# Last block of a four-layer kernel: routing rows loaded whole behind each tile's weights, another order of low parts at the changes of pass, a smaller first split

## The reference, cut to what matters

```
def _L1_ffn_ref(hidden_states, gate_weight, gate_up_weights, down_weights, shared_gate_up, shared_down):
    ...
    scores = jax.nn.softmax(x @ gate_weight.T, axis=-1)
    topk_weight, topk_idx = jax.lax.top_k(scores, TOP_K)
    y = jnp.zeros_like(x)
    for e in range(N_EXPERTS):
        w_e = jnp.sum(jnp.where(topk_idx == e, topk_weight, 0.0), axis=-1)
        y = y + w_e[:, None] * _glu_ffn(x, gate_up_weights[e], down_weights[e])
    y = y + _glu_ffn(x, shared_gate_up, shared_down)
```

## Time and profile before

| | |
|---|---|
| median of 3 runs | 1177.15 us (1173.48 to 1182.71) |
| the profiled execution | 1173.77 us |
| its span | 1172.0 us |
| PE busy | 1062.4 us (91%) |
| DVE, ACT, POOL busy | 782.4 (67%), 678.9 (58%), 519.9 us (44%) |
| mean granted TensorE clock | 0.966 of full speed |

### The profile page before, as it was taken

How to read it: one execution, slowest core, us unless ns; L and a number is a source line. 1 busy time by engine, 2 the same in 40 slices (tenths; PEclk the granted TensorE clock), 3 DMA queues, 4 the chain that set the end, 5 groups by cost and what they waited for, 6 DMA issues and landing times. The chain is left out here.

```text
span 1172.0 us, 18701 instructions
## 1 busy us (share of the span) xinstructions
PE 1062.4 (91%) x6437; PEld 816.3 (70%) x6437; DVE 782.4 (67%) x1801; ACT 678.9 (58%) x1240; POOL 519.9 (44%) x491
## 2 busy tenths in 40 slices
PE   7999999979998958499899999999789999878997
PEld 5422323246877957498799899889689787666997
DVE  6888888646666544498798999998467474222643
ACT  4577777756544444477687787787445353222444
POOL 5361421013079330476577777777406002444333
PEclk9999999999999986699899999999999999999999
DMA  3221221114236002446545456553111123544100
GB/s 84 54 60 29 48 40 28 46 35 156 73 99 124 3 3 25 67 73 122 75 60 80 75 62 83 65 71 57 14 34 37 42 56 96 149 135 138 55 19 19
DMA packets 112279, 75.98 MB, mean 65 GB/s; under 512 B 29765, under 2 KB 100633, under 8 KB 112185
## 3 DMA queue, kind: packets, MB, share of 16 engines
q1 hardware_dynamic: 111888, 74.55, 31.2%
q10 hardware_dynamic: 296, 0.23, 0.1%
HBM read 65.51 MB, written 1.28 MB: 57 GB/s over the span
## 5 line engine op out<-in xcount | busy, mean ns | idle before, releaser
L700 DVE TENSOR_REDUCE attn_row_max<-attn_rows_q 128x1 f32<-128x512 f32 x256 | 159.0, 682 | 27.3 <-PE attn_rows_q L468 26.0
L603 ACT ACTIVATE attn_probs<-attn_rows_k 128x512 f32<-128x512 f32 x256 | 136.7, 602 | 42.6 <-PE attn_rows_k L478 42.4
L2782 POOL TENSOR_TENSOR late_mids<-late_mids,early_lin_w_v 128x512 f32<-128x512 f32 x44 | 56.8, 1296 | 131.1 <-DMA early_lin_w_v<-top_weights 131.1
L478 PE MATMUL attn_rows_k<-attn_q_stack,attn_k_stack 99*128 99x512 bf16 x256 | 95.3, 380 | 1.8 <-ACT attn_probs L603 1.7
L468 PE MATMUL attn_rows_q<-attn_k_stack,attn_q_stack 96*128 96x512 bf16 x256 | 95.8, 383 | 0.9 <-DMA attn_k_stack<-attn_part 0.5
L2684 DVE TENSOR_TENSOR late_mids<-late_mids,late_bank 128x512 f32<-128x512 f32 (+1 forms) x50 | 34.3, 686 | 79.1 <-PE late_bank L80 76.1
L78 PE MATMUL late_bank<-net_x_part_low,late_w_T 128*128 128x512 f32 (+1 forms) x200 | 81.7, 408 | 0.0
L79 PE MATMUL late_bank<-net_x_part_low,late_w_T 128*128 128x512 f32 (+1 forms) x200 | 79.7, 398 | 0.0
L80 PE MATMUL late_bank<-net_x_part_low,late_w_T 128*128 128x512 f32 (+1 forms) x200 | 79.4, 397 | 0.0
L468 PEld LDWEIGHTS attn_rows_q<-attn_k_stack,attn_q_stack 96*128 96x128 bf16 x256 | 24.7, 97 | 74.2 <-DVE attn_row_max L700 47.3
L1455 POOL TENSOR_TENSOR gold_mids<-gold_mids,gold_weight 128x512 f32<-128x512 f32 x32 | 52.1, 1668 | 45.6 <-DMA gold_weight<-gold_weights 45.6
(11 more groups left out here) (397 smaller groups left out, 3317.3 us busy)
## 6 DMA issues: line engine op xcount, KB each, us to landing
lin_mix<-decay_sums SPq DMA_DIRECT2D x16, 512.0 KB, 15.5
lin_q_dec<-decay_sums SPq DMA_DIRECT2D x16, 512.0 KB, 20.3
gold_weight<-gold_weights SPq DMA_DIRECT2D x16, 256.0 KB, 3.4
early_lin_w_v<-top_weights SPq DMA_DIRECT2D x16, 256.0 KB, 3.3
s_raw_ring<-in_L_ffn_Wg SPq DMA_DIRECT2D x12, 256.0 KB, 3.1
s_raw_ring<-in_L_ffn_Wu SPq DMA_DIRECT2D x12, 256.0 KB, 3.6
gold_raw_w_down<-in_L_ffn_Wd SPq DMA_DIRECT2D x1, 2048.0 KB, 12.6
early_lin_w_q<-in_L_attn_Wq SPq DMA_DIRECT2D x16, 128.0 KB, 18.0
```

The source lines that it names most:

```text
L478: pe.matmul(ps_k[n % 3][:, :], k_stack[0:QROWS + MROWS, h, t * P:(t + 1) * P], q_stack[0:QROWS + MROWS, h, b * HALF:(b + 1) * HALF], start ...
L603: act.activation(probs[:, kk % PB, b * HALF:(b + 1) * HALF], ps_k[n % 3][:, :], ACT.Exp)\
L700: dve.tensor_reduce(row_max[:, r, b:b + 1], ps_q[n % 3][:, :], axis=AX, op=ALU.max)\
L2782: pool.tensor_tensor(out, out, weight[v % ROW_RING], ALU.mult).then_inc(weighted, 1)
```

## The change

1. **Routing rows.** `load_rows` takes a whole routing tile, 1024 tokens (4 KB per partition), in place of a half. One call stands behind each `load_tile` from tile 13 on, then ten are left. There are still two buffers, now of a whole row each: one is `lin_w_v` made one tensor; the other is the space of the fourth `w_T` buffer.
2. **Ring.** `w_T` has three buffers from tile 4 on (`slot_of`); the fourth holds tile 3, then routing rows, and is the fourth buffer of the down projection's splits again. Its first use there (pass 0, tile 3) waits on ACT until routing tile 20, the last one whose rows lie in it, is weighed: `act.wait_ge(weighted, 2 * RT - 2)`.
3. **First split.** `o_part` splits Wo in parts of 1, 3, 4, 4, 4 heads.
4. **Changes of pass.** Two low parts, not one, stand ahead of the first `dve_first` and `pool_first` of passes 1 and 2.

```
-        w_T = [s.sb(f"w_T{b}", [P, 2, 2, DK, P], F32R) for b in range(W_RING)]
+        w_T = [s.sb(f"w_T{b}", [P, 2, 2, DK, P], F32R) for b in range(W_RING - 1)]
+        raw_space, w_T_last = over(nc, s, "w_T_last", [P, 2, 2, DK, P])
+        w_T.append(w_T_last)
...
-        weight = [r[:, :, :].rearrange("p k d -> p (k d)") for r in row_space]
+        weight = [raw_space[:, :, :, :, :].rearrange("p q m k f -> p (q m k f)"),
+                  row_space[:, :, :, :].rearrange("p b k d -> p (b k d)")]
...
-        sum_parts = [[w_T[b][:, q, :, :, :].rearrange("p m k f -> p (m k f)") for q in range(2)] for b in (1, 2, 3, 0)]
+        sum_parts = [[w_T[b][:, q, :, :, :].rearrange("p m k f -> p (m k f)") for q in range(2)] for b in range(W_RING)]
...
+        O_CHUNKS = [slice(0, 1), slice(1, 4), slice(4, 8), slice(8, 12), slice(12, LH)]
+        O_AT = {c.start: n for n, c in enumerate(O_CHUNKS)}
...
+            return i if i < FIRST else (i - FIRST) % (W_RING - 1)
...
-                def load_rows(v):
-                    tile, h = divmod(v, 2)
-                    if v >= ROW_RING:
-                        sp.wait_ge(weighted, v - ROW_RING + 1)
+                def load_rows(tile):
+                    if tile >= ROW_RING:
+                        sp.wait_ge(weighted, 2 * (tile - ROW_RING + 1))
                     for e, r, k, rows in expert_pieces(tile):
-                        sp.dma_start(weight[v % ROW_RING][rows, :],
-                                     w_dram[e:e + 1, h * HALF:(h + 1) * HALF].to_broadcast((k, HALF)))\
-                            .then_inc(row_loaded[v % ROW_RING], 16)
+                        sp.dma_start(weight[tile % ROW_RING][rows, :], w_dram[e:e + 1, :].to_broadcast((k, T)))\
+                            .then_inc(row_loaded[tile % ROW_RING], 16)
...
                     if i >= ROWS_FROM:
-                        for _ in range(3):
-                            if v < 2 * (i - ST):
-                                load_rows(v)
-                                v += 1
-                for v in range(v, 2 * RT):
-                    load_rows(v)
+                        load_rows(i - ROWS_FROM)
+                for tile in range(NTILE - ROWS_FROM, RT):
+                    load_rows(tile)
...
-                    if u < W_RING:
-                        act.wait_ge(up_done, AT[(NTILE - W_RING + u, 1)] + 1)
+                    if u < W_RING - 1:
+                        act.wait_ge(up_done, AT[NTILE - W_RING + 1 + u, 1] + 1)
+                    elif u < W_RING:
+                        act.wait_ge(weighted, 2 * RT - 2)
...
-                    if i >= W_RING:
-                        act.wait_ge(up_done, AT[i - W_RING, 1] + 1)
+                    if i >= FIRST:
+                        back = FIRST if i < FIRST + W_RING - 1 else W_RING - 1
+                        act.wait_ge(up_done, AT[i - back, 1] + 1)
...
                 sum_low(1, 1)
+                sum_low(1, 3)
                 last.dve_first(dve, 0, sum_used, NTILE)
+                sum_low(1, 5)
                 last.dve_first(dve, 1, sum_used, NTILE)
...
-                        if p == 1 and n in (0, 2):
-                            last.pool_first(pool, n // 2)
+                        if p == 1 and n in (2, 4):
+                            last.pool_first(pool, n // 2 - 1)
```

More of the change, by code:

```diff
@@ L2357, in late_block, with slot_of, row_count @@
         SUM_DVE = [[True] * NTILE, [n % 2 == 1 for n in range(NTILE)], [n % 2 == 1 for n in range(NTILE)]]
+        O_CHUNKS = [slice(0, 1), slice(1, 4), slice(4, 8), slice(8, 12), slice(12, LH)]
+        O_AT = {c.start: n for n, c in enumerate(O_CHUNKS)}
         ROWS_FROM = 13
+        def slot_of(i):
+            return i if i < FIRST else (i - FIRST) % (W_RING - 1)
         def load_count(i):
             return 16 * sum(len(list(tile_loads(TILES[j], weights))) for j in range(i + 1) if j % LOAD_RING == i % LOAD_RING)
-        def row_count(v):
-            return 16 * sum(len(list(expert_pieces(j // 2))) for j in range(v + 1) if j % ROW_RING == v % ROW_RING)
+        def row_count(tile):
+            return 16 * sum(len(list(expert_pieces(j))) for j in range(tile + 1) if j % ROW_RING == tile % ROW_RING)
         def low_count(on_dve, p, n, mine):
@@ L2439, in out_unit @@
                         pe.wait_ge(out_low_pool, low_count(OUT_DVE, p, n, False))
-                    if p == 0 and n % 4 == 0:
-                        pe.wait_ge(o_split, n // 4 + 1)
+                    if p == 0 and n in O_AT:
+                        pe.wait_ge(o_split, O_AT[n] + 1)
                     _, parts = out_source(p, n)
@@ L2488, in glu @@
                     v = AT[i, h]
-                    cols, w = slice(h * HALF, (h + 1) * HALF), w_T[i % W_RING]
+                    cols, w = slice(h * HALF, (h + 1) * HALF), w_T[slot_of(i)]
                     pe.wait_ge(w_split, i + 1)
@@ L2579, in tile_high @@
                     act.wait_ge(w_turned, i + 1)
-                    if i >= W_RING:
-                        act.wait_ge(up_done, AT[i - W_RING, 1] + 1)
-                    act.activation(w_T[i % W_RING][:, 0, :, :, 0:rows], ps_w[:, :, :, 0:rows], ACT.Copy).then_inc(w_high, 1)
+                    if i >= FIRST:
+                        back = FIRST if i < FIRST + W_RING - 1 else W_RING - 1
+                        act.wait_ge(up_done, AT[i - back, 1] + 1)
+                    act.activation(w_T[slot_of(i)][:, 0, :, :, 0:rows], ps_w[:, :, :, 0:rows], ACT.Copy).then_inc(w_high, 1)
                     act.wait_ge(d_turned, i + 1)
@@ L2639, in _ @@
                     if i == NTILE - 1:
-                        for n in range(W_RING - 1):
+                        for n in range(W_RING - 2):
                             sum_part(0, n)
@@ L2645, in _ @@
                 for p in range(len(PASSES)):
-                    for n in range(W_RING - 1 if p == 0 else 0, NTILE):
+                    for n in range(W_RING - 2 if p == 0 else 0, NTILE):
                         sum_part(p, n)
@@ L2670, in tile_low @@
                 def tile_low(i):
-                    rows, w = TILE_ROWS[i], w_T[i % W_RING]
+                    rows, w = TILE_ROWS[i], w_T[slot_of(i)]
                     dve.wait_ge(w_high, i + 1)
@@ L2779, in weigh @@
                     out = product_of(tile + ST, h)
-                    pool.wait_ge(row_loaded[v % ROW_RING], row_count(v))
+                    pool.wait_ge(row_loaded[tile % ROW_RING], row_count(tile))
                     pool.wait_ge(up_taken, AT[tile + ST, h] + 1)
-                    pool.tensor_tensor(out, out, weight[v % ROW_RING], ALU.mult).then_inc(weighted, 1)
+                    pool.tensor_tensor(out, out, weight[tile % ROW_RING][:, h * HALF:(h + 1) * HALF], ALU.mult).then_inc(weighted, 1)
                 for n in range(3, 13):
@@ L2838, in network @@
             lin_wq, lin_wk = ([early.sb(f"lin_w_{m}{b}", [P, DK, HD]) for b in range(2)] for m in "qk")
-            lin_wv = [early.sb(f"lin_w_v{b}", [P, DK, 2 * HD]) for b in range(2)]
+            lin_wv_both = early.sb("lin_w_v", [P, 2, DK, 2 * HD])
+            lin_wv = [lin_wv_both[:, b, :, :] for b in range(2)]
             lin_taps = early.sb("lin_taps", [P, 2, LH, TAPS + 1])
```

34 lines of the change are left out of this document (17 added, 17 removed).

## The result

The changed kernel takes **1165.07 us** (median of 19 runs, 1156.67 to 1170.09), the kernel before 1176.67 (19 runs, 1169.32 to 1182.71): ratio **0.9895**, 95% interval 0.9876 to 0.9914, so 10 to 15 us faster. The profiled execution took 1165.97 us (span 1164.2, granted clock 0.959). It lies 7.8 us under that of before: 10.1 us are gained in the changed block, and 2.3 are lost in the untouched block ahead of it (the granted clock is 0.66 from 843 to 853 us; before it is 1.00 from 843 to 850). So I read the block alone, in two stretches: **A**, from ACT's first split of Wo to the first matmul of `sum_unit`, and **B**, from there to the end of the span. Before, A is 238.6 us and B 82.4; after, A is 215.8 and B 95.05. The gain is in A (22.8), a loss of 12.6 in B takes more than half of it back.

The account below looks back on a forecast made before the run. A ring of SP, DMA and POOL sets the pace and PE pays. 21.2 - 7.1 - 1.7 + 1.3 + 0.6 = 14.3 us off 1173.77 gives 1159.5; the median lies 3.4 above, 1162.8; given as 1161 (1154 to 1169).

Parts of the forecast that it names:

- a landing beyond 5 us: Sign against the forecast: 512 KB row loads were to land in 3.3 to 4.8 us; longer would make it wrong.
- Part 1: Tile loads in the loop: with the new order, PE's late turns 13 to 24 give back all 21.2 us.
- SP isn't held: Loop's load queue: the row load's wait is over in time, leaving about 6 us spare per tile load.
- Part 2, the stall: Down projection, pass 0, unit 3: it waits until routing tile 20 is weighed, so PE idles 7.1 us.
- The period: Row loading and weighing after the loop: one buffer's turnover with whole rows was to take 6.5 us.
- The hand-over: From tile 20 weighed to unit 3's start: splits of 0.63 and 0.69 us, plus 0.15 of hand-overs.
- X: Row loads: the extra landing time for 256 KB more, taken as 0.7 us, between 0 and 1.5.
- a cost per piece: Row loads: 43 GB/s with 512-byte pieces against 172 with longer ones speaks for a cost per piece and small X.
- rival A: Rows land in proportion to their bytes, X from 1.5 to 3.3 us; middle 1167 us, chance 0.21.
- The clock: Behind unit 3's stall: PE's granted clock averages 0.72 for 6 us, a loss of 1.7 us.
- Part 3: First split of Wo: 256 columns in place of 1024 let PE start sooner, 1.3 us gained.
- Part 4: Changes of pass: unit 2 is on time, units 4 and 6 lose less in all, 0.6 us gained.

Follow-up runs that it names:

- e3_halves: The kernel before with two half rows behind each tile's weights in place of three: 1156.59 us, ratio 0.9816.
- e4_pace: The kernel after with rows of one and of two tiles in turn behind each tile's weights, in place of one: 1153.08 us, ratio 0.9797.
- e1_own_space: The kernel after with the down projection's fourth pair of parts over the natural buffers, so unit 3 waits for no weighing: 1150.81 us, ratio 0.9782.
- e2_filled: The kernel after with 27 matmuls, written to a bank nobody reads, ahead of unit 3's wait: 1166.30 us, ratio 0.9899.
- e8_pieces: The kernel after with each row load as two DMAs of half rows (2 KB pieces) into the same buffer: 1163.73 us, ratio 0.9896.
- e7_filled46: The kernel after with 46 matmuls, written to a bank nobody reads, ahead of unit 3's wait: 1161.72 us, ratio 0.9879.
- e6: e1_own_space with the order at the two changes of pass as in the kernel before: 1151.78 us, ratio 0.9800.
- e10: The kernel after, unchanged, run again: 1159.82 us, ratio 0.9880.
- e9_halves_rest: e3_halves with the first split of Wo and the changes of pass as in the kernel after: 1149.26 us, ratio 0.9778.

## Why the prediction was right, and where its terms were off

It gave 1161 (1154 to 1169) and 0.65 for faster by over 1%; 1165.1 with a ratio of 0.9895 is that, by little. Its mechanisms came one by one; the sum of 14.3 us was too high by 4.2: the stall was 4.25 longer than forecast, and the smaller misses cancel. Two of its own signs went against it: PE's wait was to be 4 to 10 us and took 11.1, and a landing beyond 5 us was to show it wrong. One came, tile 11's 5.8 us; it delayed the start of the weighing once, while the landings behind it, which set the period, took 3.3 to 3.8.

- **Part 1 (+21.2).** 21.4 by e3_halves. Turns are 6.27 us apart. The reason as given, an order that makes SP wait with the tile loads behind it, is shown by e3_halves and made sharper by e4_pace. "SP isn't held" was too strong: it waits 8.9 us for POOL in the loop, at no cost.
- **Part 2, the stall (-7.1).** The mechanism is shown (e1_own_space), the size is not: 11.35. Three steps failed. Tile 12 was done at 1054.98, 0.53 us behind turn 24, where I had it 1.3 ahead: +1.8, the late landing of tile 11's rows. The period was 6.85, not 6.5: 4 x 0.35 = 1.4. The hand-over was taken as 1.5 with an undisturbed low part of 0.69; it took 1.73, since POOL weighs tile 21 at the same time: +1.0. Together that is 11.3. In e2_filled, where the first and the third are as I had them, the wait with its filling is 8.7.
- **X (0.7).** One whole row lands in 3.3 to 3.5 us, where halves took 3.1 in the same stretch, so X is 0.2 to 0.4; nearer to the lower bound. The view of DMA issues, 1060 to 1090 us, of before (one line) and of after:
```profile
early_lin_w_v<-top_weights SPq DMA_DIRECT2D x3, 256.0 KB, 3.1
```
```profile
late_raw_w_T_last<-top_weights SPq DMA_DIRECT2D x1, 512.0 KB, 3.5
early_lin_w_v<-top_weights SPq DMA_DIRECT2D x1, 512.0 KB, 3.3
```
  The period is longer all the same (6.85, not 6.5), because a tile that lies in two experts needs two loads, issued one behind the other, and because weighing takes up to 2.99 us beside DVE's splits. Both were left out. That 6.5 came so near 6.85 is partly luck: X was too large by 0.3 to 0.5, and what was left out made up for it. The argument "a cost per piece", from 43 and 172 GB/s, is refuted by e8_pieces; rival A needed a landing longer by 1.5 us or more, which these rows exclude.
- **The clock (-1.7).** 2.4 here. That idle time brings it is shown by e7_filled46 against after. The step that failed is the size: PE was idle so long that the clock had fallen before unit 3, and the low stretch lasted to about 1090.3. The Trainium skill, page "TensorE: Matmul & The Clock Gate", section "HAM oscillation — how this bites in real kernels", says that the work behind such a wait starts cold; the first matmul of 0.58 us agrees (0.39 behind the wait of e7_filled46, at full clock). By that rule the loss was sure, and behind waits of this length it came each time; behind shorter ones it is a matter of chance (below).
- **Part 3 (+1.3).** 1.2 to 1.4. That the clock might then not fall at the start came true in three profiles out of nine with this split (e1, e6, e10: A is 214.6) and in the other six didn't: 1.2 to 1.5 us, by chance. That is less than the 1.7 given.
- **Part 4 (+0.6).** 1.1. Unit 4 waits 0.90 us in both passes, as foreseen; the loss at unit 6 that I had added didn't come.
- **Sum.** 21.4 - 11.35 - 2.4 + 1.4 + 1.1 = 10.15, the 10.1 us between the two profiled blocks. The medians say 11.6; they also hold the blocks ahead, whose clock moves from run to run.

## What to carry to other kernels

When a queue holds loads that wait for a slow consumer, compare the turnover of its buffers with the period of the loop: in the orders run here the loads behind them starved only where more was queued per period than is turned over, and then one number in the order was the whole remedy. Before a buffer is shared to make transfers larger, ask when its last user is done; here that cost 13.75 us at the pace chosen, and even where it costs nothing (e4_pace) it bought nothing over half rows (e9_halves_rest). And give a split on DVE its length beside a working POOL, not its length alone, where both its inputs lie in SBUF.

## What the runs showed of the hardware that was not expected

- **DVE and POOL slow each other.** A low part of 128x512 takes 0.69 us alone and up to 1.80 beside POOL's multiplications; a pair of these takes 2.48 to 2.54 us alone and 2.95 to 3.6 beside DVE's low parts. Beside DVE's work in the loop, of which one input lies in a bank, a pair stays at 2.52 to 2.56. The Trainium skill, page "SBUF — State Buffer", section "SBUF: two separate sides", says that of a DVE instruction with two SBUF inputs and a GpSimd instruction that reads SBUF, the one that starts first holds a shared pair of ports for its whole length while the other is blocked; the traces agree in direction, with both engines paying.
- **The clock falls or doesn't behind equal waits.** After 3.27 us of idle time at the block's start it fell six times in nine (in after, e2, e7 and e8 it had been low shortly before as well); after 1.56 at the second change of pass it stayed in before and e3_halves and fell in e6_changes; after 2.25 it fell in e2_filled, after 1.21 it stayed in e7_filled46. Two starts of the block, of e4_pace and of e1_own_space, in which PE did the same in the 12 us ahead, at a clock of 1.00:
```profile
852.00:858.00 6.00, 5.15 (x29) 5.04 (x30) 5.21 (x8) 4.41 (x8) 0.00 (x0) 0.72 0.55 159
```
```profile
852.00:858.00 6.00, 4.05 (x32) 3.95 (x33) 5.18 (x8) 5.33 (x9) 0.00 (x0) 1.00 0.60 153
```
  They have 0.72 and 1.00 of the full clock behind the same 3.27 us. Behind waits of 1.5 to 3.3 us such a term belongs in the range, at 1.2 to 1.7 us, not in the sum.
- **A load's rate goes by how much moves at once.** Row loads of 256 KB that moved one behind the other showed 172 GB/s over 1 us; two of them at once reached 336, and one of 512 KB 369 and 410, each in its fullest half microsecond.
